# Two-layer graph network on one core: the piece-widening split, the start of the second edge sum and one 64-input layer

## What is computed

```python
edge_index = jnp.stack([src, dst])
h = jnp.maximum(_layernorm(x), 0.0)
# L0: two sums over edges
agg = segment_sum(h[src], dst); h = relu(relu((h + agg) @ W1 + b1) @ W2 + b2)
agg = segment_sum(h[src], dst)                               # 128 features
x = x + relu((h + agg) @ W3 + b3) @ W4 + b4
h = jnp.maximum(_layernorm(x), 0.0)
# L1: one network on each node, a sum over edges, another network
y = relu(relu(h @ WM1 + bM1) @ WM2 + bM2) @ WM3 + bM3        # WM1 is 64 x 128
z = segment_sum(y[src], dst)                                 # 64 features
x = x + relu(relu(concat(h, z) @ WU1 + bU1) @ WU2 + bU2) @ WU3 + bU3
```

## Time and profile before

| | us |
|---|---|
| median of 3 runs (lowest, highest) | 1017.05 (1016.2, 1017.14) |
| the profiled execution, its own time | 1016.0 |
| its span in the trace | 1014.2 |
| TensorE matmul busy in the span | 919.9 (91%) |
| VectorE busy | 685.0 (68%) |
| ScalarE busy | 696.9 (69%) |
| GpSimd busy | 225.0 (22%) |
| mean granted TensorE clock | 0.983 of 2.4 GHz |

### The profile page before, as it was taken

One profiled execution on the slowest core, in us unless ns is written; L12 is line 12 of the kernel. 1 busy time (PEld: TensorE's weight loads), 2 busy tenths in 40 slices (PEclk: granted clock), 3 DMA queues, 4 the chain that ended last, 5 costly groups with the idle time before them and its releaser, 6 DMA issues.

```text
span 1014.2 us, 25298 instructions
## 1 busy us (share of the span) xinstructions
PE 919.9 (91%) x11325; PEld 735.5 (73%) x11325; DVE 685.0 (68%) x745; ACT 696.9 (69%) x664; POOL 225.0 (22%) x120
## 2 busy tenths in 40 slices
PE   0169999999999999889999999999999799999996
PEld 0158888888888888448778777777777676676765
DVE  6999999999999996476744444444444445455452
...
GB/s 102 14 76 141 120 111 123 142 132 112 107 140 133 133 102 104 96 4 152 122 120 111 111 126 110 112 122 111 126 111 46 114 172 220 220 214 222 216 207 41
DMA packets 81216, 126.78 MB, mean 125 GB/s; under 512 B 9776, under 2 KB 57904, under 8 KB 80976
## 3 DMA queue, kind: packets, MB, share of 16 engines
...
q0 software_dynamic: 3136, 3.22, 1.4%
...
## 4 chain that ended last, share of the span: by engine, by line
PE 49%; ACT 5%; issue 3%; DVE 2%; DVEq 0%; ACTq 0%
PE net_ps_hi L917 14%; PE net_ps_lo L917 14%; PE net_ps_hi L930 9%; PE net_ps_m L871 7%; ACT net_wide L803 5%; PE net_ps_f L871 2%; PE net_ps_hi L871 1%; PE net_ps_t L879 1%; PE net_ps_t L958 1%; PE net_ps_lo L901 0%; DVE keys L756 0%; ACT net_hid L806 0%; DVE net_high L650 0%; DVE net_first L653 0%; DVE net_xT L641 0%
## 5 line engine op out<-in xcount | busy, mean ns | idle before, releaser
L803 ACT ACTIVATE net_wide<-net_raw 128x3584 fp32r<-128x3584 fp8e4 (+1 forms) x104 | 311.3, 3020 | 88.8 <-PE net_ps_lo L917 83.4
L402 ACT ACTIVATE build_cnts<-build_ps_cnt 128x784 fp8e4<-128x784 f32 (+1 forms) x400 | 299.4, 821 | 52.4 <-PE build_ps_cnt L464 47.1
L917 PE MATMUL net_ps_hi<-net_wide,net_first 128*128 128x512 f32 (+1 forms) x637 | 251.5, 398 | 2.4 <-DVE net_first L653 2.4
L480 PE MATMUL build_ps_out<-build_parts,build_cnts 128*128 128x198 bf16 x2401 | 242.6, 250 | 0.0
L917 PE MATMUL net_ps_lo<-net_wide,net_first 128*128 128x512 f32 (+1 forms) x637 | 242.5, 384 | 0.0
L293 DVE TENSOR_TENSOR build_hot_lo<-build_grid_lo,build_keys_t 128x4096 bf16<-128x4096 bf16 x100 | 228.6, 2286 | 2.1 <-ACT build_keys_t L390 1.6
L480 PEld LDWEIGHTS build_ps_out<-build_parts,build_cnts 128*128 128x128 fp8e4 x2401 | 197.8, 98 | 8.0
L597 DVE CAST net_wide<-net_raw 128x3584 fp32r<-128x3584 fp8e4 (+1 forms) x78 | 149.5, 1917 | 76.1 <-PE net_ps_lo L917 37.3
L930 PE MATMUL net_ps_hi<-net_wide,net_second 128*128 128x512 f32 (+1 forms) x637 | 159.1, 401 | 13.8 <-ACT net_wide L803 12.9
L930 PEld LDWEIGHTS net_ps_hi<-net_wide,net_second 128*128 128x128 f32 x637 | 115.4, 191 | 53.8 <-ACT net_wide L803 25.2
L464 PE MATMUL build_ps_cnt<-build_hot_a,build_hot_lo 64*128 64x49 bf16 x6272 | 124.0, 184 | 29.5 <-DVE build_hot_a L293 24.3
...
## 6 DMA issues: line engine op xcount, KB each, us to landing
...
build_rows<-in_dst_rows,build_row_i POOLq DMA_INDIRECT x49, 4.3
build_edges<-in_edges,build_start_i POOLq DMA_INDIRECT x49, 5.2
...
```

What stands on the lines that cost most here:

```text
L402: nc.scalar.activation(cnts[u % A_RING][:, 0:n, :, 8 * k:8 * k + 8], ps_cnt[b % CNT_RING][:, 0:n, 0:8 * NW].rearrange("p t (n a) -> p t a ...
L480: last = nc.tensor.matmul(ps_out[w % 2][:, 0:3 * FX], cnts[u % A_RING][:, w % 2, c, :], parts64[:, c, :, :].rearrange("p t f -> p (t f)"), ...
L803: expand(act, lambda to, x: nc.scalar.activation(to, x, ACT.Identity), e).then_inc(grown["act"], 1)
L917: last = nc.tensor.matmul(ps[b % 2][:, 0:n * P], first[:, c, lo:lo + H], expanded[e % WIDE_RING][:, 0:n, k, :], start=(c == 0), stop=(c == ...
```

## The change

It has five parts.

1. **Widening.** `EXPAND` is turned round: VectorE widens pieces 0, 2, 4, 6 of each block, ScalarE 1, 3, 5. The very first piece is widened by VectorE between the splits of blocks 10 and 11 of the first network.
2. **Start of the first sum.** TensorE no longer waits for all 13 splits before it; with 12 of 13 done it starts, and only piece 6 waits for the last. The two pairs of sum buffers change places (`(b + 1) % 2`).
3. **Start of the second sum.** Its first six pieces are issued between the last block's network steps; only piece 6 waits for the last `y_split`. The loops over the two sums become one on each engine.
4. **WM1.** The copied rows are split on VectorE into `h1_parts` (high part on partitions 0 to 63, rest on 64 to 127), the weights are held twice (on both halves of the partitions) and split once into `wm[0]`, `wm[1]`; the product is two fp32r matmuls of 128 input rows in place of one fp32 product of 64.
5. **Check.** GpSimd tallies the keys (12 instructions for each of 7 pieces of 448 elements, each waiting for the one before; 24,990 elements a partition in all, counting what each writes), and VectorE only compares (`compare`, ahead of piece 20 of the first sum). Two more weight loads are queued on SyncE in the build.

```diff
-EXPAND = counts_of([("act", "dve")[(e % PIECES) % 2] for e in range(2 * BLOCKS * PIECES)])
+EXPAND = counts_of([("dve", "act")[(e % PIECES) % 2] for e in range(2 * BLOCKS * PIECES)])
...
+        h1_parts = sb("h1_parts", [P, 512], FP32R)
+        wm_high = sb("wm_high", [P, H], I32)
+        wm = [sb(f"wm{i}", [P, H], FP32R) for i in range(2)]
...
+                for i in range(PIECES):
+                    w = slice(i * PIECE, (i + 1) * PIECE)
+                    inside, source = tagged[:, 0, :, :], tagged[:, 1, :, :]
+                    nc.gpsimd.tensor_scalar(inside, keys[:, 1, w, :], float(NW), None, ALU.is_lt)
+                    link(nc.gpsimd.tensor_scalar(source, keys[:, 1, w, :], 0.0, None, ALU.is_ge))
+                    link(nc.gpsimd.tensor_tensor(inside, source, inside, ALU.mult))
+                    link(nc.gpsimd.tensor_scalar(source, keys[:, 1, w, :], float(P), None, ALU.mult))
+                    link(nc.gpsimd.tensor_tensor(source, source, keys[:, 0, w, :], ALU.add))
+                    link(nc.gpsimd.tensor_tensor(source, source, inside, ALU.mult))
+                    for half in (32, 16, 8, 4, 2):
+                        link(nc.gpsimd.tensor_tensor(tagged[:, :, :, 0:half], tagged[:, :, :, 0:half], tagged[:, :, :, half:2 * half],
+                                                     ALU.add))
+                    nc.gpsimd.tensor_tensor(tally[:, 0:2, w], tagged[:, :, :, 0], tagged[:, :, :, 1], ALU.add).then_inc(tallied, 1)
+                    pool.wait_ge(tallied, i + 1)
...
+                v.tensor_scalar(wm_high[:, :], W["L1_gnn_WM1_twice"][:, :].bitcast(I32), -4096, None, ALU.bitwise_and).then_inc(wm_ready, 1)
+                dve.wait_ge(wm_ready, 1)
+                v.tensor_copy(wm[0][:, :], wm_high[:, :].bitcast(FP32)).then_inc(wm_ready, 1)
+                v.tensor_tensor(wm[1][:, :], W["L1_gnn_WM1_twice"][:, :], wm_high[:, :].bitcast(FP32), ALU.subtract).then_inc(wm_ready, 1)
...
+                    for e in pieces(0)[0:AHEAD]:
+                        if s == BLOCKS and EXPAND[e][0] == "dve":
+                            grow(e)
...
-                            v.tensor_tensor(xT[:, 0:n * P], ps_hi[b % 2][:, 0:n * P], hT[:, columns(b)], ALU.add).then_inc(x_half, 1)
+                            v.tensor_tensor(xT[:, 0:n * P], ps_hi[(b + 1) % 2][:, 0:n * P], hT[:, columns(b)], ALU.add).then_inc(x_half, 1)
-                            v.tensor_tensor(xT[:, 0:n * P], xT[:, 0:n * P], ps_lo[b % 2][:, 0:n * P], ALU.add).then_inc(x_ready, 1)
+                            v.tensor_tensor(xT[:, 0:n * P], xT[:, 0:n * P], ps_lo[(b + 1) % 2][:, 0:n * P], ALU.add).then_inc(x_ready, 1)
...
+                            dve.wait_ge(h1_copied, b + 1)
+                            if b:
+                                dve.wait_ge(y_split, b)
+                                dve.wait_ge(product_m1, b)
+                            else:
+                                dve.wait_ge(split_done, BLOCKS)
+                            flat = high[0:F, :, :].rearrange("p w f -> p (w f)")[:, 0:n * P]
+                            v.tensor_scalar(flat, hT[0:F, columns(b)].bitcast(I32), -4096, None, ALU.bitwise_and).then_inc(h1_high, 1)
+                            dve.wait_ge(h1_high, b + 1)
+                            v.tensor_copy(h1_parts[0:F, 0:n * P], flat.bitcast(FP32))
+                            v.tensor_tensor(h1_parts[F:P, 0:n * P], hT[0:F, columns(b)], flat.bitcast(FP32),
+                                            ALU.subtract).then_inc(h1_split, 1)
...
+                def compare():
+
+                    dve.wait_ge(tallied, PIECES)
+                    dve.wait_ge(check_consts, 2)
...
+                for e in [*pieces(0), *pieces(1)]:
+                    if e + AHEAD < pieces(1).stop and EXPAND[e + AHEAD][0] == "dve":
+                        grow(e + AHEAD)
+                    if e == 2 * PIECES + 6:
+                        compare()
+                    if e == 4 * PIECES:
+                        flag_rest()
+                    b, i = e // PIECES - 1, e % PIECES
+                    if b < BLOCKS:
+                        stage1(b, i)
+                    else:
+                        stage2(b - BLOCKS, i)
+                    if e == pieces(1)[PIECES - 1]:
+                        stage1(BLOCKS, 0)
+                for i in range(PIECES):
+                    stage2(BLOCKS - 1, i)
...
-                pe.wait_ge(relu_b, BLOCKS)
-                pe.wait_ge(split_done, BLOCKS)
...
+                    if b == 0:
+                        pe.wait_ge(split_done, max(BLOCKS - 1, -(-(i + 1) * PIECE // 4)))
+                    if i == 0 and b == 1:
+                        pe.wait_ge(relu_b, BLOCKS)
...
+                    if i == 0 and b < 2:
+                        pe.wait_ge(x_ready, BLOCKS - 1 + b)
                     if i == 0 and b >= 2:
                         pe.wait_ge(z_ready, b - 1)
+                    if b == 0:
+                        pe.wait_ge(y_split, BLOCKS if i == PIECES - 1 else BLOCKS - 2)
...
-                            pe.wait_ge(h1_copied, b + 1)
-                            mm(ps_m[:, 0:n * P], W["L1_gnn_WM1"][:, :], hT[0:F, columns(b)]).then_inc(product_m1, 1)
+                            pe.wait_ge(h1_split, b + 1)
+                            for k in range(2):
+                                last = nc.tensor.matmul(ps_m[:, 0:n * P], wm[k][:, :], h1_parts[:, 0:n * P], start=(k == 0), stop=(k == 1))
+                            last.then_inc(product_m1, 1)
...
 
-                for number, use, stage in ((0, use1, stage1), (1, use2, stage2)):
-                    for e in pieces(number):
-                        use(e)
-                        stage((e // PIECES) % BLOCKS - 1, e % PIECES)
-                    for i in range(PIECES):
-                        stage(BLOCKS - 1, i)
-                    if number == 0:
-                        stage(BLOCKS, 0)
-                        pe.wait_ge(y_split, BLOCKS)
+                for e in pieces(0):
+                    use1(e)
+                    stage1(e // PIECES - 1, e % PIECES)
+                for i, e in enumerate(pieces(1)):
+                    if i == PIECES - 1:
+                        stage1(BLOCKS - 1, i)
+                        stage1(BLOCKS, 0)
+                    use2(e)
+                    if i < PIECES - 1:
+                        stage1(BLOCKS - 1, i)
+                    elif i >= PIECES:
+                        stage2(i // PIECES - 1, i % PIECES)
+                for i in range(PIECES):
+                    stage2(BLOCKS - 1, i)
...
+                    if name == "L1_gnn_WM1":
+                        for half in range(2):
+                            sp.dma_start(W["L1_gnn_WM1_twice"][half * F:(half + 1) * F, :], a[name]).then_inc(loaded, 16)
```

106 lines of the change are left out of this document (41 added, 65 removed).

## The result

The changed kernel takes **1000.12 us** (median of 4 runs, 999.83 to 1002.69); the kernel before, in the same runs, 1017.1. The ratio is 0.9838, 95% interval 0.9819 to 0.9857, 1.6% less time and clear of no change. Forecast was 999.0. The profiled execution took 999.83 us with a span of 998.0; before, 1016.0 and 1014.2.

The account below looks back on a forecast made before the run. TensorE was taken to bound the first sum, ScalarE the second. Terms -8.7 - 9.7 + 0.8 + 1.2 + 0.2 - 2.8 + 1.0 = -18.0 took the profiled 1016.0 to 998.0, median 999.0 us; range 991 to 1007.

Parts of the forecast that it names:

- WM1's pair: First sum: two fp32r matmuls take 0.46 us instead of 1.25, saving 0.79 a block, -8.7 us over eleven full blocks.
- VectorE widens four: Second sum: ScalarE no longer binds, z comes 0.52 us late, blocks 14.39 instead of 15.36 us, -9.7 over ten.
- The last full block's +0.8: End of second sum: narrow pieces and z behind a narrow CAST, about 13.0 us to WU1 of block 11, was 12.2.
- Start of the first sum: VectorE's first widening, 2.03 us ahead of split 12, starts TensorE +1.2 us later; weight operations add +0.2.
- The three weight operations: Operations ahead of the first network's first copy, forecast to cost +0.2 us.
- GpSimd: Check moved to GpSimd beside the first network: VectorE's casts and first widening wait for it, +1.0 us taken.
- rival C: GpSimd blocks VectorE: first-network casts and the tail wait up to 0.6 us each; doubled, +6, 1004 us; chance 0.09.
- list of signs against it: Signs of a wrong forecast: blocks at 15, DMA waits, VectorE waiting for `tally`, first-network casts longer than 0.43 us.
- The passage: Between the sums: early pieces hidden, ScalarE's widening ahead of the last ReLU; WU1 of block 0 at 827.05, -2.8 us.
- A: Second sum: counts come too late by DMA, blocks stay near 15.4 us, total 1008.7 us; chance 0.10.
- B: z not late in the second sum (ten times 0.5) or passage's ReLU slips in first (3.7): 990.3 us; chance 0.10.
- D: First sum: `compare` waits near 530 us for GpSimd's tally if above 4.8 ns an element; 1069 us; chance 0.05.

Follow-up runs that it names:

- the experiment: WM1 as one fp32 product again, splits of h1 and weight left out, against the changed kernel: 1009.96 us, ratio 0.9937.
- the eleventh experiment: Against the changed kernel, three orders turned round (z before widening, last ReLU before widening, first two pieces exchanged) and GpSimd's tally moved into the second sum: 1005.72 us, ratio 0.9808.
- the twelfth experiment: The two loads of the 64-row weight issued behind all other weight loads, against the changed kernel: 1011.55 us, ratio 0.9878.
- the experiments that brought it about: Two edits, each against the changed kernel: z before piece 2's widening, 1003.17 us, ratio 0.9834; last ReLU before ScalarE's widening in the passage, 1008.02 us, ratio 0.9877.

## Why the prediction was right, step by step

The forecast, -18.0, stands against -16.2 by the profiled execution it was summed against. The two steps that carry it, WM1 and the widening, came by the mechanism stated. The errors of single terms, -0.4, +1.7, +1.2, -0.2 and -0.5 (the end, which had no term), cancel in part, and the total lies nearer (999.0 forecast, 1000.12 measured) than they would let one expect. That nearness is luck: the same kernel took 1009.1 on another chip. Its steps:

- **WM1's pair**: -8.7 forecast, -9.1 measured over W3 of block 0 to 11. The surcharge was read rightly, and 0.84 us a block in the experiment instead of 0.79. Cover for the split held in the full blocks; at the narrow pieces behind them WM1 waited 0.87 us, forecast 1.0.
- **VectorE widens four**: -9.7 forecast, -8.0 measured. The wait for z was put at 0.52 us a block. By the starts of the products it is 0.61, and what the step left out is that WU1 behind a wait takes 0.10 longer: 0.70 in all, blocks of 14.57, not 14.39. The last full block's +0.8 came as +0.77.
- **Start of the first sum**: +1.2 and +0.2 forecast and +1.0 for GpSimd, 2.4 together. Measured +3.63: the build +1.01; up to the first split +0.83 (14.33 us in, before 13.50); first to last split +2.60; and -0.82, since the first product no longer waits for the 13th split. The widening's part in the 2.60 is 1.7; with the -0.82 it makes +0.9, where +1.2 was forecast. The +0.83 is mostly the tally: 0.36 by the weight subtraction of 0.64 us instead of 0.28, 0.40 by the first split's cast of 0.83 us instead of 0.43. The low clock lasts 6.8 us in both kernels there, so under 0.1 us is left for it, unless the terms overlap: the eleventh experiment, with no tally there and the same 6.8 us, still has 13.74. The three weight operations do not delay the first copy by themselves, where +0.2 was forecast. Why the build took 1.01 longer stays open: the loads may have a part, but the twelfth experiment does not show it, and the build varies by more than this with the same code.
- **GpSimd**: +1.0 forecast, for waits of VectorE. In the profiled execution 0.9 between the splits (34.13 - 33.26) and 0.76 ahead of them, 1.6 together; between the splits 0.5 to 2.4 in others. The mechanism is the one that rival C gave, VectorE's casts wait for GpSimd's instruction; a cast longer than 0.43 us stood in the prediction's own list of signs against it, although the +1.0 supposes just that. The 0.6 more that I had set as bound for one cast was exceeded: by 0.68 here, by 0.95 in others. The whole came to 1.6 and not to rival C's 6, since eight of twelve casts were hit, six of them for less than 0.6.
- **The passage**: -2.8 forecast, -3.03 measured. Shifted by the 5.5 us that the first sum gained, the forecast's times lie within 0.6 us throughout: the ReLU released at 817.9 (818.3), piece 6 at 819.7 (820.3), WU1 at 826.7 (827.05). The low clock that the step put at four microseconds lasts 3.4 (814.1 to 817.5); before it lasted 10.2. Inside the step one wait was sized wrongly: TensorE stood 1.55 us for ScalarE's widened piece 5, where some tenths were forecast, and 5.9 us over the four waits near the passage's end, where some 5 were.

Of the rivals, A did not come: in the second sum's windows the queues move 229 GB/s, and neither TensorE nor VectorE waits for a transfer there. B was not true of this kernel, but its prices were near: the experiments that brought it about gave 0.70 a block (forecast 0.5) and 2.9 us (3.7). C was true in mechanism, 1.6 us in size instead of 6: the casts are hit in some blocks only, and blocks with idle time on VectorE hide it. D did not come: the tally takes 93 us for 24,990 elements, 3.7 ns each, under the 4.8 from which it decides, and `compare` waits for nothing. The eleventh run showed it at work when the tally was late, with 8.5 us of TensorE.

The Trainium skill, SBUF — State Buffer, "SBUF: two separate sides", describes an exclusive lock between VectorE and GpSimd, held for a whole instruction. The trace agrees: VectorE's SBUF-to-SBUF casts are lengthened (0.43 to 1.11 us) and end 0.28 us behind the GpSimd instruction within which they began, while its subtractions out of PSUM stay at 0.68, and GpSimd's passes are lengthened as VectorE widens more (1.33 to 3.7 us). The Trainium skill, GPSIMD Engine Reference, "Performance versus the Vector engine", states about half of VectorE's rate, from which 65 us was estimated for the tally; the trace has 93, the waits for VectorE among them.
